# First pair of a 7x7 dilated convolution by channel block over seven banks, with its filter preparation started on a half load

## The reference, cut to what matters

```python
# x: (4, 256, 64, 64), all fp32
k = conv(x, w1 (128,256,7,7), padding 6, dilation 2) + b1
k = conv(k, w2 (49,128,1,1)) + b2
attn = softmax(k, axis=1)                      # 49 weights per pixel
xp = pad(x, 6)
x1 = einsum('bkchw,bkhw->bchw', 49 shifts of xp by 2u, 2v, attn)
h = relu(bn(conv1x1(x1, v1)))                  # 256 -> 64 channels
h = relu(bn(conv3x3(h, v2)))
out = relu(bn(conv1x1(h, v3)) + x1)            # 64 -> 256 channels
```

## Time and profile before

| what | value |
|---|---|
| time, median of 3 runs | 867.92 us (866.33 to 868.16) |
| the profiled execution's own time | 868.58 us |
| its span (first to last instruction) | 866.8 us |
| TensorE busy | 811.2 us (94%) |
| VectorE busy | 649.2 us (75%) |
| ScalarE busy | 376.1 us (43%) |
| GpSimd busy | 346.7 us (40%) |

### The profile page before, as it was taken

One profiled execution on the slowest core, in us unless ns is written; L12 is line 12 of the kernel. 1 busy time (PEld: TensorE's weight loads), 2 busy tenths in 40 slices (PEclk: granted clock), 3 DMA queues, 4 the chain that ended last, 5 costly groups with the idle time before them and its releaser, 6 DMA issues.

```text
span 866.8 us, 13972 instructions
## 1 busy us (share of the span) xinstructions
PE 811.2 (94%) x5084; PEld 770.1 (89%) x5084; DVE 649.2 (75%) x884; ACT 376.1 (43%) x647; POOL 346.7 (40%) x256
## 2 busy tenths in 40 slices
PE   4998988999999999999999999999968989996896
PEld 4997988999999999999999999999968867775685
DVE  4895888898699589868968977896576667129796
ACT  1332112334343434434344444534246697116396
POOL 3318586385267248527723852772200010006200
PEclk9999999999999999999999999999989989998999
DMA  9920515986894996779499688747299995020598
GB/s 265 372 104 0 98 28 132 218 215 171 185 244 123 230 180 193 202 162 243 120 242 174 183 208 168 206 114 211 65 257 264 267 335 236 0 84 14 187 425 358
DMA packets 249932, 162.18 MB, mean 187 GB/s; under 512 B 191833, under 2 KB 232778, under 8 KB 247178
## 3 DMA queue, kind: packets, MB, share of 16 engines
q1 hardware_dynamic: 241162, 144.52, 63.6%
q10 hardware_dynamic: 8704, 16.78, 6.1%
HBM read 99.48 MB, written 56.36 MB: 180 GB/s over the span
## 4 chain that ended last, share of the span: by engine, by line
PE 75%; DVE 8%; issue 5%; POOL 5%; ACT 3%; DMA 3%; SPq 1%; ACTq 0%; DVEq 0%; POOLq 0%
PE ps L1090 21%; PE ps L1092 21%; PE ps L1091 21%; PE ps L1160 4%; PE ps L1176 3%; PE ps L1208 3%; POOL xbuf L778 2%; PE ps L1115 1%; POOL ring L767 1%; DMA w1raw<-in_L_conv_w 1%; DMA raw<-bands 1%; DVE y L1842 1%; POOL whole L762 1%; DVE whole L1519 1%; DVE wsum L1471 1%
## 5 line engine op out<-in xcount | busy, mean ns | idle before, releaser
L767 POOL TENSOR_TENSOR ring<-whole,ring 128x576 fp32r<-128x576 f32 x112 | 188.5, 1687 | 272.9 <-ACT ring L848 272.9
L1090 PE MATMUL ps<-w_hi,ring 128*128 128x336 f32 x832 | 277.7, 334 | 9.4 <-DVE me L1596 7.2
L1092 PE MATMUL ps<-w_hi,ring 128*128 128x336 f32 x832 | 265.3, 319 | 0.0
L1091 PE MATMUL ps<-w_lo,ring 128*128 128x336 f32 x832 | 264.2, 318 | 0.0
L1090 PEld LDWEIGHTS ps<-w_hi,ring 128*128 128x128 f32 x832 | 159.9, 192 | 10.2 <-issue 7.7
L1091 PEld LDWEIGHTS ps<-w_lo,ring 128*128 128x128 f32 x832 | 159.6, 192 | 0.0
L1092 PEld LDWEIGHTS ps<-w_hi,ring 128*128 128x128 f32 x832 | 158.7, 191 | 0.0
L848 ACT ACTIVATE ring<-whole 128x576 fp32r<-128x576 f32 x112 | 87.1, 778 | 107.1 <-POOL whole L762 58.1
L848 ACT ACTIVATE band_hi<-ps 128x320 fp32r<-128x320 f32 (+1 forms) x128 | 53.0, 417 | 127.5 <-PE ps L1160 121.3
L1519 DVE SCALAR_TENSOR_TENSOR whole<-xbuf 128x576 f32<-128x576 f32 x80 | 88.3, 1105 | 14.6 <-POOL ring L767 7.5
L1090 PE MATMUL ps<-band_hi,xT_hi 128*128 128x224 f32 (+2 forms) x320 | 94.9, 297 | 3.2 <-DVE band_lo L1431 3.1
(11 more groups left out here) (165 smaller groups left out, 1370.2 us busy)
## 6 DMA issues: line engine op xcount, KB each, us to landing
xq<-in_x SPq DMA_DIRECT2D x116, 256.0 KB, 4.9
raw<-bands SPq DMA_DIRECT2D x32, 768.0 KB, 7.1
xbuf<-in_x SPq DMA_DIRECT2D x16, 1024.0 KB, 8.7
x_dram<-x ACTq DMA_DIRECT2D x32, 512.0 KB, 4.7
x1in<-x_dram SPq DMA_DIRECT2D x7, 2048.0 KB, 13.3
bands<-wide SPq DMA_DIRECT2D x64, 199.0 KB, 5.4
out<-x1in SPq DMA_DIRECT2D x12, 1024.0 KB, 5.9
w1raw<-in_L_conv_w SPq DMA_DIRECT2D x2, 3136.0 KB, 12.7
```

Of the source, the lines that this page charges most:

```text
L767: pool.tensor_tensor(split(k, 1), positions(whole[:, k % TBUFS, :], 0, 2), split(k, 0).bitcast(F32), ALU.subtract).then_inc(sig_lo_done, 1)
L1090: pe.matmul(dst, l_hi, r_hi_, start=first, stop=False, **kw)
L1091: pe.matmul(dst, l_hi, r_lo_, start=False, stop=False, **kw)
L1092: return pe.matmul(dst, l_lo, r_hi_, start=False, stop=last, **kw)
```

## The change

The first pair takes its chunks by channel block (all seven points of block 0, then all of block 1) and gives each point its own bank. Its sums all move to q = 1 (eleven of them) and to part 0 of q = 2 (the last six: MHALF's four, C_ZERO, C_INF). In pair 1 HALF1 uses bank 3, and MHALF then waits for C_DIFF. `c_of` of the first four x tiles moves from GpSimd to VectorE as one instruction. w1's first channel block is loaded in two halves of 64 input channels from ScalarE's queue, and the first four columns are made in two passes of 64 output rows each; SyncE waits for the first half before it loads x. The copies of columns 7, 8 and 9 and the low part of column 7 move up ahead of the last sums of block 0. Image 0's parts in q = 3 move from part 4 on to part 6 on.

```diff
+FIRST = [(point, cb) for cb in range(CB) for point in (TWO, ONE, MINUS, HALF1, MHALF, ZERO, INF)]
+FIRST_BANKS = {TWO: 0, ONE: 1, MINUS: 2, HALF1: 3, MHALF: 4, ZERO: 5, INF: 6}
+EARLY = 4
+def order_of(s):
+    return ORDER if s else FIRST
+def bank_of(s, point):
+    if s == 0:
+        return FIRST_BANKS[point]
+    return 3 if (s, point) == (1, HALF1) else BANKS[point]
...
-                return {4: (0,), 5: (1, 2), 6: (3, 4), 7: (5,), 8: (6, 7), 9: (8,), 10: (9, 10), 11: (11,), 12: (12, 13), 14: (14,)}.get(part, ())
+                return {6: (0,), 7: (1, 2), 8: (3, 4), 9: (5, 6), 10: (7, 8), 11: (9, 10), 12: (11, 12), 13: (13,), 14: (14,)}.get(part, ())
...
+        W1_PARTS = [(0, 0, MID0 // 2), (0, MID0 // 2, MID0), (1, 0, MID0)]
+        def load_w1(eng, i):
+            kb, lo, hi = W1_PARTS[i]
+            eng.dma_start(w1raw[:, kb, lo:hi, :]..., w1[:, kb * P + lo:kb * P + hi, :, :]...).then_inc(w1_loaded[i], 16)
...
-            for kb in range(CB):
-                sp.dma_start(w1raw[:, kb, :, :] ...)   # x(0), x(1) after kb == 0
+            sp.wait_ge(w1_loaded[0], 16)
+            for i in range(CB):
+                load_x(i)
+            load_w1(sp, 2)
             load_x(2)
...                                                      # GpSimd
+            pool.memset(ident[:, :], 0.0).then_inc(consts, 1)
+            pool.wait_ge(consts, 1)
+            diagonal(ident[:, :], 1.0, 0)
-                    if i and k == chunk_at(i // 2, TWO, i % 2) - RING + 4:
+                    if i >= EARLY and k == chunk_at(i // 2, TWO, i % 2) - RING + 4:
                         c_of(i)
...                                                      # ScalarE
+            for i in range(2):
+                load_w1(act, i)
...
+            for i in range(CB * K):
+                cb, v = divmod(i, K)
+                if not K <= i < K + 3:
+                    column(i)
+                if i == 3:
+                    sig_hi(0)
+                if (cb, v) == (0, 6):
+                    sig_hi(1)
...
                 if v == 6:
                     for j in range(5, 10):
+                        if cb == 0 and j in (5, 7):
+                            for ahead in (K, K + 1) if j == 5 else (K + 2,):
+                                column(ahead)
                         whole_hi(len(WHOLES) * cb + j)
...                                                      # TensorE
+            def weff(i, lo, hi):
+                kb, v = divmod(i, K)
+                for p in range(K):
+                    mm = pe.matmul(psW[i % 4][lo:hi, p * KP:(p + 1) * KP], w1raw[:, kb, lo:hi, (K - 1 - p) * K + v], w2T[:, :],
+                                   start=True, stop=True)
+                return mm
+            pe.wait_ge(w1_loaded[0], 16)
+            for i in range(4):
+                weff(i, 0, P // 2)
...
+            pe.wait_ge(w1_loaded[1], 16)
+            for i in range(4):
+                weff(i, P // 2, P).then_inc(weff_done, 1)
...
+                    elif cb == 0 and s == 1:
+                        before = {TWO: comb(0, C_HALF - 1), ONE: comb(0, C_ONE), MINUS: comb(0, C_DIFF), HALF1: comb(0, C_MHALF - 1),
+                                  MHALF: comb(1, C_DIFF), ZERO: comb(1, C_HALF - 1), INF: comb(1, C_ONE)}
+                        pe.wait_ge(comb_done, before[point])
...                                                      # VectorE
+                    if (cb, v, n) == (0, 6, 1):
+                        direct_lo(1, 0)
+            def c_of(i):
+                dve.wait_ge(b_done, i + 1)
+                a, b = (xflat(i)[:, o:o + SH * XC] for o in (0, 4))
+                minus(a, b, a).then_inc(c_done, 2)
+                if (cb, v) == (0, 3):
                     a_of(0)
                     b_of(0)
+                    c_of(0)
                 if (cb, v) == (1, 0):
                     signal(3)
-                    a_of(1)
-                    b_of(1)
+                    signal(4)
...
+                combos = ({} if q == 0 else
+                          {4: (C_ONE,), 6: (C_SUM, C_DIFF), 8: (C_TWO, C_TWO + 1, C_TWO + 2), 9: (C_TWO + 3,), 10: (C_HALF, C_HALF + 1),
+                           12: (C_HALF + 2, C_HALF + 3)} if q == 1 else ...
+                        if (q, part) == (0, 8):
+                            a_of(1)
+                            b_of(1)
+                        if (q, part) == (2, 0):
+                            for i in range(C_MHALF, COMBOS):
+                                combine(0, i)
+                        if (q, part) in ((0, 11), (2, 1), (2, 7)):
+                            c_of(1 if q == 0 else 2 + part // 7)
```

More of the change, by code:

```diff
@@ L732, in _, with diagonal @@
         def _(pool):
-            for t in (ident[:, :], gavg[:, :], up[:, :, :], dn[:, :, :], smx[:, :, :]):
+            def diagonal(t, value, off):
+                pool.affine_select(out=t, in_=t, compare_op=ALU.not_equal, fill=value, base=off, pattern=[[-1, P]],
+                                   channel_multiplier=1).then_inc(masked, 1)
+            pool.memset(ident[:, :], 0.0).then_inc(consts, 1)
+            pool.wait_ge(consts, 1)
+            diagonal(ident[:, :], 1.0, 0)
+            for t in (gavg[:, :], up[:, :, :], dn[:, :, :], smx[:, :, :]):
                 pool.memset(t, 0.0).then_inc(consts, 1)
@@ L741, in _ @@
             pool.wait_ge(consts, 11)
[L744 to L750, removed]
+            for i, off in enumerate((0, 64, -64)):
+                pool.wait_ge(masked, i + 1)
+                diagonal(gavg[:, :], 0.5, off)
+            pool.wait_ge(masked, 4)
             pool.memset(wide[:, :, :, :], 0.0).then_inc(zeroed, 1)
@@ L864, in whole_hi, with column @@
                 copy(w_hi[:, cb, WHOLES[j], :], wsum[:, i % 3, :]).then_inc(wsum_hi_done, 1)
-            for i in range(CB * K):
+            def column(i):
                 cb, v = divmod(i, K)
@@ L988, in half @@
                         exponentials(soft)
-                    if part % 2 and conv is not None and 0 < first + part // 2 < NCHUNK - RING + 2:
+                    if part % 2 and conv is not None and 1 < first + part // 2 < NCHUNK - RING + 2:
                         sig_hi(first + part // 2 + RING - 2)
@@ L1101, in _ @@
             pe.wait_ge(prep_dve, 3)
-            pe.matmul(psB[:, 0:KP], b1bc[:, :], w2T[:, :], start=True, stop=False)
-            pe.matmul(psB[:, 0:KP], ones[:, :], b2row[:, :], start=False, stop=True).then_inc(prep_pe, 1)
-            for i in range(CB * K):
+            pe.matmul(psB, b1bc[:, :], w2T[:, :], start=True, stop=False)
+            pe.matmul(psB, ones[:, :], b2row[:, :], start=False, stop=True).then_inc(prep_pe, 1)
+            pe.wait_ge(w1_loaded[1], 16)
+            for i in range(4):
+                weff(i, P // 2, P).then_inc(weff_done, 1)
+            pe.wait_ge(prep_dve, 4)
+            for i in range(4, CB * K):
                 kb, v = divmod(i, K)
-                if v == 0:
-                    pe.wait_ge(w1_loaded[kb], 16)
-                if i == 3:
-                    pe.wait_ge(prep_dve, 4)
+                if i == K:
+                    pe.wait_ge(w1_loaded[2], 16)
                 if i >= 4:
@@ L1113, in _ @@
                         pe.wait_ge(wlo_done, len(DIRECT) * ((i - 4) // K) + sorted(DIRECT).index((i - 4) % K) + 1)
-                for p in range(K):
-                    mm = pe.matmul(psW[i % 4][:, p * KP:(p + 1) * KP], w1raw[:, kb, :, (K - 1 - p) * K + v], w2T[:, :],
-                                   start=True, stop=True)
-                mm.then_inc(weff_done, 1)
+                weff(i, 0, P).then_inc(weff_done, 1)
             def conv_part(k, part):
```

95 lines of the change are left out of this document (48 added, 47 removed).

## The result

The changed kernel takes 871.10 us (median of 7 runs, 869.42 to 873.17); the kernel before, run beside it, 867.92 (866.33 to 869.06). The ratio is 1.0044, with a 95% interval of 1.0031 to 1.0058: slower by 0.4%, where the prediction had 857.2 and held the time within 850.5 to 865.0. Its profiled execution has a span of 869.2 us, against 866.8.

A forecast was written before the change was run, and what follows sets the result against it. TensorE, busy 94% of the span, was taken as the bound. Start -4.0, first pair -5.8, pair 1 -1.9 and image 0 +1.0 gave -10.7 us, so 857.2 from 867.9; range 850.5 to 865.

The forecast's parts named there:

- the three signs: Passes stepping at 0.22 us, a w1raw stop between 18 and 31 us, PE gaps over 1 us from 143 to 165.
- Start: Folding before chunk 0: half loads and half-width passes bring chunk 0 to 52.2 us from 56.2, -4.0 us.
- The rival of full-price half passes: First four columns: half passes still cost 0.22 us a record, +12.0 us, 869.2 in all; chance 0.12.
- The stop for C_DIFF at chunk 21: Pair 1: TensorE stops 4.7 us for VectorE's C_DIFF, 6.2 with the clock stretch.
- The list: VectorE's work from C_SUM of pair 0 to C_DIFF of pair 1: 43.85 us, from 89.7 to 133.5.
- The first pair, -5.8: Chunks 0 to 14: the stop for C_ONE and its clock stretch go, chunk 14 at 102.8 us, -5.8 us.
- Cover: 4 us: Chunk 8: its signal and low part ready at about 78 us, 4 us before it starts at 82.
- Pair 1, -1.9: Pair 1: old stops worth 8.1 us go, a new one at chunk 21 costs 6.2; net -1.9 us.
- The rival "collisions": VectorE and GpSimd wait out each other's instructions, lengthening VectorE's list by 5 us: 862 us; chance 0.15.
- Image 0, +1.0 (0 to 4): q = 3: 15 parts of work packed into nine, nearly covered, costing +1.0 us (0 to 4).
- 19 us of work against 21: Image 0's stretch: VectorE's about 19 us of work nearly covered by TensorE's 21.
- The tail, 0: From chunk 28 on nothing differs, TensorE has no gap, and the shift is kept to the end: 0.

The follow-up runs named there:

- e4: The kernel before with only the new start (w1 in two halves, two passes, ident first), copies of columns 7 to 9 not moved up; 867.85 us, ratio 1.0011.
- e8: e7 with c_of(1) on VectorE also made to wait for the low part of chunk 8; 860.93 us, ratio 0.9919.
- e1: The changed kernel with image 0's parts in q = 3 back from part 4 on, as before the change; 863.22 us, ratio 0.9948.
- e6: The changed kernel with image 0's parts from part 5 on; 867.15 us, ratio 0.9993.
- e7: e1 with signal 20 ahead of softmax and C_ONE, C_SUM, C_DIFF of pair 1 ahead of c_of(3); 860.98 us, ratio 0.9915.
- e3: e1 with c_of(2) and c_of(3) back on GpSimd; 866.32 us, ratio 0.9988.
- e9: e7 with signal 21 and pair 1's C_ONE, C_SUM, C_DIFF ahead of the end of softmax; 862.75 us, ratio 0.9948.
- e10: e9 with c_of(3) and signal 22 also ahead of the end of softmax; 867.70 us, ratio 0.9993.
- e2: The changed kernel with c_of(2) and c_of(3) back on GpSimd; 873.31 us, ratio 1.0063.

## Why the prediction was wrong

Of the three signs that the prediction named for being wrong one came: TensorE stands still 2.47 us between 143 and 165 us. And it had no stop before 100 us, where there are two, 0.39 and 2.09.

**What held.** *Start:* -4.0 predicted, -3.7 measured; the record with 64 columns 6.44 / 56 = 0.115 us (0.11 predicted), the first half landed before 7.43 (7.8), chunk 0 at 52.50 (52.2). The rival of full-price half passes is excluded. *Copies moved up:* e4 shows the 2.2 us that they save. *The stop for C_DIFF at chunk 21* came, from VectorE's list as named, 2.1 us in place of 4.7. *The list:* from C_SUM (94.61) to the end of C_DIFF (141.09) it is 46.5 us, 43.85 predicted; this is partly luck, as shown under pair 1.

**The first pair, -5.8; measured -2.3.** The failing step is "Cover: 4 us" for chunk 8, which took durations without collisions. VectorE's filters of block 1 ended 4.5 us later than in the sum (3.2 of it already at the end of block 0's, 48.72 us), `b_of(1)` took 2.44, `c_of(1)` 3.54, GpSimd's low part 2.75. The low part for chunk 8 was ready at 84.95, predicted 78. The stops of 0.39, 2.09 and 0.94 us (chunk 14's for a sum, not in the sum at all) are 3.4 of the 3.5 us. e8 takes 1.3 us of the first two away and does not begin chunk 14 earlier. That the collisions and the late filters are what made the low part late is read from the traces; apart from e8 no run separates them.

**Pair 1, -1.9; measured +1.8.** The failing step is C_DIFF at 133.5, the end of VectorE's list. It came at 141.09, 7.6 us late, and chunk 22 began at 146.6 where the sum had 139.1; 3.8 us of that were lost before chunk 14. Two things make the 7.6. The list began 4.9 us later than I had it (C_SUM at 94.61, not 89.7), which follows from chunk 8 and a signal ahead of it. And it was 2.65 us longer: two signals in two steps took 2.5 us each in place of 1.55, and `b_of` twice 2.45 in place of 1.4, which was the minimum of the earlier trace rows (their median is 1.9); these 4 us were half hidden, since softmax with signal 20 took 8.0 us (125.41 to 133.41) where I had 10.05. A second thing was missed by reading the list only at its end: signal 20 stood in it behind the top of softmax, and I did not ask when its low part is due. In TensorE's account the miss is the stops, 3.11 + 2.14 where 4.7 was predicted, and the low clock, 10.2 us x (1 - 0.155 / 0.28) = 4.6 us where I had one stretch, 1.5; 3.6 us together. But chunk 20's stop is not a cause of its own: chunk 21's wait covers it, as the rows of e1 and e6 show. That the order of the list sets chunks 21 and 22 is shown by e7, which moves signal 20 and C_DIFF together and is 3.9 us further ahead at chunk 22 than e1; the share of each move is not. The rival "collisions" was right about the sign and about the mechanism, but it had 5 us and 862 us in all, and was given 0.15.

**Image 0, +1.0 (0 to 4); measured +5.4.** The reason, "19 us of work against 21", compares sums over the stretch. The bound was in single positions: low parts of 0.5 us behind `a_of` of 2.6. Against the places of the kernel before the new ones cost 6.2 us (e1_parts is at -5.0 where the changed kernel is at +1.2; with the tail 8.1 at the end of the traces and 8.3 by the ratios), and e6 lies between: this is shown. That the range of this term ended at 4 was an argument by sums too.

**The tail, 0; measured +1.8.** "From chunk 28 on nothing differs" holds to chunk 111 at 1.2 us (TensorE of the kernel before and after is the same there). Behind it the clock near 640 us fell for longer. The window of 620 to 670 us of the changed kernel is shown above; e7_early's:

```profile
620.00:670.00 50.00, 40.41 (x293) 38.09 (x292) 34.92 (x63) 28.70 (x61) 2.16 (x4) 0.93 0.94 257
```

A clock of 0.86 is 14 us at the low level, 0.93 is 7. TensorE's two stops between 636 and 666 us are the same in the changed kernel and in the kernel before: 6.57 us, and this one of 1.29, first in the changed kernel, then before:

```profile
655.88 0.31 PE L1125 MATMUL ps<-band_hi,xT_hi 128*128 128x96 f32 x1 [1.29 <-DVE band_lo L1491]
654.51 0.31 PE L1090 MATMUL ps<-band_hi,xT_hi 128*128 128x96 f32 x1 [1.29 <-DVE band_lo L1431]
```

Behind this short stop the clock fell again in the changed kernel (0.83 from 655 to 665 us) and not in the kernel before (1.00 from 653.9 to 663.9), and 1.5 of the 1.8 us are lost just there. e3, e9 and e10 show the second fall too and lose 2.0 us there; the six others that have 7 us there do not, nor does e2, which has 10 and no second fall. All have the same instructions here, only at other times. What decides whether the clock falls stays open; it is seen in one profiled execution of each, and no run was made to separate it. The 12 runs of e3_both lie in two groups, six from 865.3 to 865.9 us and six from 866.8 to 867.8, so a step of this size comes and goes within one kernel; that it is this fall is not shown. I count it as a spread of 2 us that no reading of the change could give.

**Together.** With start and order as built, the sum would have been about right only if the parts of image 0 had stayed and VectorE's order in q = 2 had been written for its due times. e7 and e8 are near that kernel. They end 7.0 and 7.6 us ahead where the sum had 10.7; the 3 to 4 us that are missing are about what the first pair misses.

## What to carry to other kernels

When a wait is removed by moving work to an engine that is 90% busy in that stretch, make its list with the durations that its entries have beside the other engine's work, and with a due time for every entry: here the list ended 7.6 us late, and moving two of its entries ahead gave 4 of them back. But ask of a late entry whether a later wait covers it before moving it alone. Work that looks covered in sum (19 us in 21) is not covered when pieces of 0.5 us are wanted at once behind pieces of 2.6. And a lead is worth something only up to the next round trip with a fixed length, here 12.4 us from softmax's end to `raw`.

## What the runs showed of the hardware

- An fp32 record with 64 stationary columns took 0.115 us with 48 moving columns, half of the 0.22 with 128 columns. Both are at the lower clock: the conv matmuls right behind the folding start 0.28 us apart until 56.6 us in the changed kernel, although the profile's stretches print 1.00 for the time before (its record of the clock begins at 56.6).
- A VectorE instruction with two SBUF inputs and a GpSimd one stretched each other: 2.55 to 3.54 us and 1.39 to 2.75 us. The rule of the Trainium skill ("SBUF — State Buffer", section "Who interferes with whom") has one wait for the other's end; here GpSimd's instruction began at 82.20 and ended 1.24 us after VectorE's end at 83.71, which agrees. `c_of(1)` had met the end of a GpSimd signal (80.15, 1.15 us) at its own start.
- Four scatters of 199 KB to DRAM and the reload of 768 KB from it, first issue to use, took 12.4 us in e10_late and 12.2 in e9_sums.
- The time at the low clock near 640 us varied between kernels with the same instructions there, 6.8 to 13.6 us, and behind stops of about 3.3 us at chunk 21 it was 0 in e7_early and 6.8 us in e8_c1.
